# Eighteen passes instead of nineteen: a group's attention laid across two halves of the software pipeline

## The reference

```python
x = _layernorm(x + L0(x, adj))   # five small two-layer GCNs on subsets of the first 25 nodes, fused
x = _layernorm(x + L1(x, adj))   # 8-head attention, scores + log(adj + 1e-6), softmax, output projection
x = _layernorm(x + L2(x, adj))   # relu(D^-1/2 adj D^-1/2 (x W^T + b))
x = _layernorm(x + L3(x, adj))   # 5 gated layers:
    A = (adj != 0)
    for l in range(5):
        m = h @ weight[l];  agg = A^T @ m;  h = gru_cell(agg, h)   # gates r, z, n
```

## Time and profile before

| | |
|---|---|
| median of 3 runs | 1730.95 us (1729.19 to 1732.3) |
| the profiled execution's own time | 1731.32 us |
| its span, first to last instruction | 1729.5 us |
| TensorE busy | 1622.2 us, 94% of the span |
| VectorE / ScalarE / GpSimd busy | 79% / 76% / 45% |
| TensorE weight loads busy | 77% |
| granted TensorE clock over the span | 0.982 of full speed |

### The profile page before, as it was taken

The page is one execution under the profiler, slowest core; times in us unless marked ns, Lnnn a source line. Parts: engine busy times, 40 slices in busy tenths (PEclk is TensorE's granted clock), DMA queues, the critical chain, the costliest instruction groups (busy, mean ns, idle before and its releaser), DMA issues.

```text
span 1729.5 us, 33712 instructions
## 1 busy us (share of the span) xinstructions
PE 1622.2 (94%) x12060; PEld 1328.9 (77%) x12060; DVE 1365.5 (79%) x3531; ACT 1313.4 (76%) x3122; POOL 779.8 (45%) x843
## 2 busy tenths in 40 slices
PE   4779999999999999999999999999999999999984
PEld 3567788787878878787887878788787878877763
DVE  5577897878789787878978787897978789787753
ACT  1467788787778878777887877788787778887763
POOL 2233454535445453544545354454535445453432
PEclk8799999999999999999999999999999999999997
DMA  3000100101010010101001010100101010000000
GB/s 89 21 24 20 30 13 26 29 13 30 25 29 14 26 29 13 30 25 30 14 26 29 14 29 26 29 13 26 28 14 29 26 29 14 25 14 13 13 7 12
DMA packets 84800, 40.92 MB, mean 24 GB/s; under 512 B 10629, under 2 KB 84634, under 8 KB 84634
## 3 DMA queue, kind: packets, MB, share of 16 engines
q1 hardware_dynamic: 84250, 38.64, 8.1%
q10 hardware_dynamic: 384, 0.13, 0.0%
HBM read 30.36 MB, written 8.39 MB: 22 GB/s over the span
## 4 chain that ended last, share of the span: by engine, by line
PE 79%; DVE 11%; ACT 7%; issue 2%; POOL 1%; POOLq 0%; DVEq 0%; ACTq 0%
PE RA L908 17%; PE RB L908 16%; PE Q L875 8%; PE RT L1084 8%; PE RT L875 4%; PE Q L1011 4%; ACT x L510 3%; PE M L875 3%; PE Q L1026 3%; PE M L943 2%; PE M L951 2%; PE Q L994 2%; DVE stats L638 2%; PE M L1054 2%; PE Q L998 2%
## 5 line engine op out<-in xcount | busy, mean ns | idle before, releaser
L493 POOL TENSOR_TENSOR h_lo<-hT,h_hi 128x512 fp32r<-128x512 f32 x160 | 210.5, 1316 | 547.7 <-ACT h_hi L587 518.8
L565 ACT ACTIVATE e_s<-Q,s_ng 128x128 f32<-128x128 f32 x1024 | 296.8, 401 | 19.2 <-DVE s_ng L746 17.4
L496 POOL TENSOR_TENSOR hd<-hT,nn 128x512 f32<-128x512 f32 x160 | 206.2, 1289 | 35.8 <-ACT nn L599 35.7
L593 ACT ACTIVATE tr<-RA,b_rz 128x512 f32<-128x512 f32 x160 | 114.6, 716 | 101.4 <-PE RA L908 101.4
L599 ACT ACTIVATE nn<-tr,wT 128x512 f32<-128x512 f32 x160 | 117.3, 733 | 96.5 <-DVE tr L797 96.5
L752 DVE TENSOR_TENSOR p_s<-Q,adjTe 128x512 f32<-128x512 f32 x256 | 172.0, 683 | 21.7 <-PE Q L875 21.6
L746 DVE TENSOR_REDUCE s_ng<-Q 128x4 f32<-128x512 f32 x256 | 167.8, 681 | 10.1 <-PE Q L1011 8.8
L793 DVE SCALAR_TENSOR_TENSOR un<-tr,un 128x512 f32<-128x512 f32 x160 | 109.7, 685 | 73.3 <-ACT un L596 73.0
L789 DVE TENSOR_TENSOR agg_lo<-RT,agg_hi 128x512 fp32r<-128x512 f32 x160 | 109.9, 687 | 72.0 <-ACT agg_hi L590 70.1
L875 PE MATMUL Q<-ident,e_s 128*128 128x128 f32 x1024 | 156.9, 277 | 9.5 <-ACT e_s L565 9.5
L875 PEld LDWEIGHTS Q<-ident,e_s 128*128 128x128 f32 x1024 | 125.4, 142 | 34.6 <-ACT e_s L565 14.0
(11 more groups left out here) (188 smaller groups left out, 4342.9 us busy)
## 6 DMA issues: line engine op xcount, KB each, us to landing
adjn<-in_adj_dram SPq DMA_DIRECT2D x32, 256.0 KB, 2.9
xin<-in_x_dram SPq DMA_DIRECT2D x32, 256.0 KB, 3.3
adjr<-in_adj_dram SPq DMA_DIRECT2D x32, 256.0 KB, 3.1
out_dram<-x SPq DMA_DIRECT2D x32, 256.0 KB, 2.4
adjc<-in_adj_dram SPq DMA_DIRECT2D x128, 4.0 KB, 1.9
xs<-in_x_dram SPq DMA_DIRECT2D x120, 16.0 KB, 1.7
W1s<-in_L_gnn_W_dram SPq DMA_DIRECT2D x1, 640.0 KB, 4.4
W2s<-in_L_gnn_W_dram SPq DMA_DIRECT2D x2, 320.0 KB, 5.4
```

What stands on the lines that cost most here:

```text
L493: pool.tensor_tensor(h_lo[g][:, :], hT[g][:, :], h_hi[g][:, :], ALU.subtract).then_inc(SG["h_lo"][g], 1)
L496: pool.tensor_tensor(hd[g][:, :], hT[g][:, :], nn[g][:, :], ALU.subtract).then_inc(SG["hd"][g], 1)
L565: ins = act.activation(e_s[:, j, c, :], Q[j][:, c * P:(c + 1) * P], ACT.Exp, bias=s_ng[:, j, c:c + 1])
L593: act.activation(tr[g][:, :], RA[:, :], ACT.Tanh, bias=b_rz[:, 0:1], scale=0.5).then_inc(SG["r_act"][g], 1)
```

## The change

The same steps are laid out with a largest lag of 2. The attention of a group is cut after the first pair of graphs (w = 0): `te` to the first `a` stand at the end of a half, the second pair of graphs and the tail at the start of the next half. The graph convolution of the group follows in that same half, after the attention's tail, and `begin` stands at that half's end; its layers 0 to 2 come in the next half and 3 and 4 in the one after. The small GCNs are done in one half (`l0_deg` to `l0_out`) but for `l0_fuse` and `l0_add`, which come in the next. In all there are 16 + 2 = 18 passes, 36 halves, all of them used. `MERGE` is new for all four engines, `ORDER` is adapted, and the waits for the bank M2 follow the new order of its users. No instruction is added to or taken from the work of a pair.

The diff, without the strings of three engines:

```diff
--- before.py
+++ after.py
@@ -46,46 +46,48 @@
     r_act=LAYERS, u_act=LAYERS, n_act=LAYERS, z_act=LAYERS, rv=LAYERS, rw=LAYERS, h_hi=LAYERS, h_lo=LAYERS, agg_hi=LAYERS, hd=LAYERS, he=LAYERS, h_new=LAYERS,
     f_mm=1, y4=1, ln4=2 * GB, ln4_eps=1, ln4_pow=1, nm4=1, x4=1,
 )
-LAG = 3
+LAG = 2
 
 MERGE = dict(
-    tensor=("AARARRRBBRABARRBRRAARAARAARRBARARBRAARRBBABRRBRBRARRARARRRBARRARAABARABRBAARRRBRRRRAARRRARABAARAAABRRRRA",
-            "AABRRARRRRARRRARRARRBAARARAAARRARARBARABARBRBRRAABRRRAAABARAARRBRARARARRBARRRRARRRRAAAARARBARARRR"),
...
+    tensor=("RABAARBRBRRABRARRRRRRBBABAARABRBRAARAABRRRRARRRAARARARBARBAABARRRBABRRBARAABRARRABRRRRARAARRBAARARBAARARRBR",
+            "ARARRRAAABBRARRAARRAAARBARARARRAAAARRRBABRAAARRARRRRABRRARRRARRBRRARRBARRRRRRARARAAARAARARARRR"),
...
 )
 
 
 def attention_steps(half):
-    at = (1, half)
-    out = [(*at, "te", 0), (*at, "x1_t", 0), (*at, "qkv", 0)]
-    for w in range(PAIRS):
-        out += [(*at, "s", w)]
+    def pair(at, w):
+        out = [(*at, "s", w)]
         for kind, j in (("max", 0), ("max", 1), ("t", 0), ("max", 2), ("t", 1), ("p", 0), ("max", 3), ("t", 2), ("p", 1),
                         ("t", 3), ("p", 2), ("p", 3)):
             out += [(*at, kind, BANKS * w + j)]
-        out += [(*at, "a", w)]
-    return out + [(*at, "u", 0), (*at, "u", 1), (*at, "n", 0), (*at, "n", 1), (*at, "on", 0), (*at, "wo", 0)]
+        return out + [(*at, "a", w)]
+
+    old, new = (1, half), (1 - half, 1 - half)
+    tail = [(*old, "u", 0), (*old, "u", 1), (*old, "n", 0), (*old, "n", 1), (*old, "on", 0), (*old, "wo", 0)]
+    return pair(old, 1) + tail + [(*new, "te", 0), (*new, "x1_t", 0), (*new, "qkv", 0)] + pair(new, 0)
 
 
 def first_third_steps(half):
-    end, last, pair = (1 - half, 1 - half), (2 - half, 1 - half), (0, 0)
-    second = [(*last, "x2_t", 0), (*last, "l2_t", 0), (*last, "l2_agg", 0), (*end, "adj_t", 0), (*end, "l0_add", 0)]
+    end, last, pair = (1 - half, 1 - half), (1, half), (0, 0)
+    first = [(*end, "adj_t", 0), (*end, "l0_add", 0)]
+    third = [(*last, "x2", 0), (*last, "x2_t", 0), (*last, "l2_t", 0), (*last, "l2_agg", 0)]
     if half == 0:
-        return [(*pair, "l0_deg", 0), (*last, "x2", 0), *second, (*pair, "l0_dinv", 0), (*pair, "l0_mask", 0), (*pair, "l0_row", 0),
-                (*pair, "l0_turn", 0), (*pair, "l0_col", 0), (*pair, "l0_nat", 0), (*end, "x1", 0),
-                (*pair, "l0_nat2", 0), (*pair, "l0_y", 0), (*pair, "l0_hid", 0), (*pair, "l0_hid", 1)]
-    return [(*pair, "l0_z", 0), (*pair, "l0_zt", 0), (*pair, "l0_out", 0), (*last, "x2", 0), (*pair, "l0_fuse", 0),
-            *second, (*end, "x1", 0)]
+        return [(*pair, "l0_deg", 0), *first, (*end, "x1", 0), (*pair, "l0_dinv", 0), (*pair, "l0_mask", 0), (*pair, "l0_row", 0),
+                (*pair, "l0_turn", 0), (*pair, "l0_col", 0), (*pair, "l0_nat", 0),
+                (*pair, "l0_nat2", 0), (*pair, "l0_y", 0), (*pair, "l0_hid", 0), (*pair, "l0_hid", 1), *third,
+                (*pair, "l0_z", 0), (*pair, "l0_zt", 0), (*pair, "l0_out", 0)]
+    return [(*pair, "l0_fuse", 0), *first, (*end, "x1", 0), *third]
 
 
 def gated_steps(half):
 
-    this, other, new = (2, half), (3 - half, 1 - half), (2 - half, 1 - half)
+    this, other, new = (2 - half, 1 - half), (2, half), (1, half)
     slots = [(*this, 0), (*other, 3), (*this, 1), (*other, 4), (*this, 2)]
     out = []
     for n, (lag, g, layer) in enumerate(slots):
@@ -383,8 +385,8 @@
                 sp.dma_start(outr[:, b0:b0 + GB, :], x4[g][:, :, :]).then_inc(out_done[g], 16)
 
 
-            ORDER = [(0, 0, "small"), (0, 1, "small"), (3, 0, "store"), (2, 1, "again"), (0, 0, "load"),
-                     (3, 1, "store"), (1, 0, "again"), (0, 1, "load")]
+            ORDER = [(0, 0, "small"), (0, 1, "small"), (0, 0, "load"), (3, 1, "store"), (1, 1, "again"),
+                     (0, 1, "load"), (2, 0, "store"), (0, 0, "again")]
 
             for g in range(NG):
                 sp.sem_inc(out_done[g], 16)
@@ -946,6 +948,8 @@
                         turn_weights() if k == 0 else multiply_weights()
                 elif kind == "l0_z":
                     wait(pe, "hid_t", it, 2)
+                    if it > 0:
+                        wait(pe, "a_relu", it - 1, 1)
                     for c in range(NK):
                         for h in range(2):
                             ins = pe.matmul(group_cols(M2, c), W2s[:, c, h, :], group_cols(hid_t[:, h, :], c), start=(h == 0), stop=(h == 1))
@@ -967,10 +971,12 @@
                     ins.then_inc(S["o_mm"], 1)
                 elif kind == "adj_t":
                     pe.wait_ge(adj_in[g], (it + 1) * 16)
-                    if it == 0:
-                        wait(pe, "o_relu", it, 1) if g == 0 else wait(pe, "y1", it, 1)
+                    if g == 0:
+                        wait(pe, "o_relu", it, 1)
+                    elif it == 0:
+                        wait(pe, "y1", it, 1)
                     else:
-                        wait(pe, "a_relu", it - 1, g + 1)
+                        wait(pe, "a_relu", it - 1, 2)
                     for q in range(GB):
                         ins = turn(M2[:, q * P:(q + 1) * P], adjn[g][:, q, :])
                     ins.then_inc(S["adjt_mm"], 1)
@@ -1043,8 +1049,10 @@
                     ins.then_inc(S["wo_mm"], 1)
                 elif kind == "x2_t":
                     wait(pe, "x2", it, g + 1)
-                    if g == 0 and it + 1 < ITERS:
-                        wait(pe, "o_relu", it + 1, 1)
+                    if it + 1 < ITERS:
+                        wait(pe, "hid_t", it + 1, 2) if g == 0 else wait(pe, "y1", it + 1, 1)
+                    else:
+                        wait(pe, "y1", it, 2) if g == 0 else wait(pe, "a_relu", it, 1)
                     for q in range(GB):
                         ins = turn(M2[:, q * P:(q + 1) * P], x2[g][:, q, :])
                     ins.then_inc(S["x2t_mm"], 1)
```

More of the change, by code:

```diff
@@ L48 @@
 )
-LAG = 3
+LAG = 2
 MERGE = dict(
-    tensor=("AARARRRBBRABARRBRRAARAARAARRBARARBRAARRBBABRRBRBRARRARARRRBARRARAABARABRBAARRRBRRRRAARRRARABAARAAABRRRRA",
-            "AABRRARRRRARRRARRARRBAARARAAARRARARBARABARBRBRRAABRRRAAABARAARRBRARARARRBARRRRARRRRAAAARARBARARRR"),
[L54 to L59, removed]
+    tensor=("RABAARBRBRRABRARRRRRRBBABAARABRBRAARAABRRRRARRRAARARARBARBAABARRRBABRRBARAABRARRABRRRRARAARRBAARARBAARARRBR",
+            "ARARRRAAABBRARRAARRAAARBARARARRAAAARRRBABRAAARRARRRRABRRARRRARRBRRARRBARRRRRRARARAAARAARARARRR"),
+    vector=("RABARABABRRRRAAARRARRRRABRRRAAARRRARRBABRBBBRBARAAAARRBRRABBBRRRABAARRAAABARBAAAARRRRRRBRRABRRRRAAAAABRRBRR",
+            "ARAAARARBABAARRRARAAARRARRRABRAAARARBRRRAARRAARABRRABRARRRARAARRBRRRAAARRBRRRRRRARRRAAARRARARR"),
+    scalar=("RBRABARBRRABRRRRAARARBRAABRBABBARBRARRBRRRAAAARAAARRARRRAABBARRRBABRRRABABRRARARBRRRRARRRAAABARRABAAARARBRR",
+            "ARAAARRRRAAAARAAARBBARRRRARAAAAABRRBARARAARRARRBRRARRRRBRABRRRRARRRRBARARRRRAAAAARAARRARRRARRR"),
+    gpsimd=("RABRARBRAARRRRRBRRRRAABRARBBBARABBRRBARAAARARRABRBARBRRRBRARAAAARBRRRRAABBRRAAAAAARRBAARABRRBAARRRABARRARRR",
+            "AAAARRRRRRRARBRRABBARRRARARABARAAARAAARRRRARAABAAARARRRRRARRABRBARARRARRRARRARRAABAARARRRRRRRA"),
 )
 def attention_steps(half):
-    at = (1, half)
-    out = [(*at, "te", 0), (*at, "x1_t", 0), (*at, "qkv", 0)]
-    for w in range(PAIRS):
-        out += [(*at, "s", w)]
+    def pair(at, w):
+        out = [(*at, "s", w)]
         for kind, j in (("max", 0), ("max", 1), ("t", 0), ("max", 2), ("t", 1), ("p", 0), ("max", 3), ("t", 2), ("p", 1),
```

## The result

The changed kernel takes 1763.51 us (median of four runs, 1763.09 to 1764.85); the kernel before, run beside it, 1731.62 (1729.19 to 1733.11). The ratio is 1.0189, with a 95% interval of 1.0177 to 1.0201: 1.9% slower. The forecast was 1758, with a range of 1722 to 1775. The sum came out right, but two terms of the pass were wrong by a microsecond each and cancelled, as the stages show.

A forecast was written before the change was run, and what follows sets the result against it. The prediction took TensorE, busy for 94% of the span, to bound the kernel. Fill and drain of 311.7 us plus 14 passes of 103.2 gave a span of 1756.5, as a median 1758, range 1722 to 1775.

The forecast's parts named there:

- Fill and drain, 311.7 + 14 P: Whole span: fill of 143.5 us, 14 complete passes of length P, drain of 168.2; P forecast at 103.2.
- the break-even of 101.3: Complete passes: the pass length P at which the changed kernel's span would equal that of the kernel before.
- The three old stalls go, 2.0 us: TensorE in each pass: waits before `u`, `qkv` and `wo` vanish because other steps now stand ahead; 2.0 us gained.
- forecast 98.4: TensorE's work in a complete pass, with the small stalls that stay: 98.4 us, bounds 98.0 and 98.9.
- `begin`, 2.5 us: End of the second half: TensorE waits for x3, three transposes covering part; 2.5 us each pass, bounds 1.9 and 3.0.
- case C: Rival: `begin` chain shorter or partly hidden, no stall between halves; P 100.0, median 1713, range 1700 to 1727; chance 0.2.
- `r0` of g0, 0.9 us: Between first and second half: `r0` waits for agg_hi behind ScalarE's queue, and for agg_lo; 0.9 us, bounds 0 and 2.
- The rest of the pass, put down as covered: All other waits in a complete pass: found covered, often with 0.1 to 0.5 us to spare.
- The clock, 1.4 us: TensorE's clock falls after the `begin` stall in six passes of ten, 2.3 us each; 1.4 per pass on average.
- case B: Rival: the clock holds in the complete passes; P 101.8, median 1738; chance 0.2.
- A: The forecast itself: stall at `begin` and a clock that falls in most passes; 1758, range 1745 to 1775; chance 0.42.

The follow-up runs named there:

- late_all: Changed kernel reordered on VectorE, ScalarE and GpSimd: x3 earlier, finished group's norm split, its output normalisation where ScalarE idles; 1733.1 us, ratio 1.0002.
- late_x3: Changed kernel with VectorE doing the attention's products p1 and p2 ahead of a_bin and nm in the second half; 1818.71 us, ratio 1.0502.
- early_x3: Changed kernel with VectorE's a_bin and shift nm of the next group ahead of the finished group's output norm, both halves; 1759.32 us, ratio 1.0165.
- late_out_only: Changed kernel with ScalarE's four normalisations of the finished group moved into the next half, where ScalarE stands idle; 1757.93 us, ratio 1.0145.
- the pairing named above: Not run: the first half of one follow-up order (52.75 us) with the second half of another (47.52), which would make a pass of 100.3.
- late_relu: Changed kernel with ScalarE's five relus of l0_out after agg_hi of layer 0 in the next half instead of ahead of it; 1781.36 us, ratio 1.0287.

## Why the forecast was right, and where its steps were not

- **Fill and drain, 311.7 + 14 P.** Held as a frame. Measured 316.3: the fill 2.5 us longer (2.2 of it before 105.2, where the forecast had 103), the drain 2.1, with the clock at 0.97 where the kernel before had 1.00. That is 4.6 of the 5.7 us by which the span is above 1756.5. In late_all, with a better order, fill and drain take 145.8 and 166.3, together 312.1; its P of 101.31 is the break-even of 101.3, and its time is that of the kernel before. So at an unchanged P of 100.8 the structure is worth 6 us with the fill and drain of late_all (312.1 + 14 x 100.8 = 1723.3, against 1729.5; the forecast had 6.6), and the order of this change keeps 2 of it (316.3 + 14 x 100.8 = 1727.5).
- **The three old stalls go, 2.0 us.** Right, but TensorE's work was mis-sized: forecast 98.4, measured 99.35. It is not work: the steps `r` take 15.8 us a pass instead of 14.7, with delays that the view counts as busy, 0.5 at `r0` of g0 and 0.4 at `r4` of g1, where each matmul starts within 0.06 us of the end of its `agg_hi` or `agg_lo`. The places where a step follows its own operand closely were not in the forecast's list of waits.
- **`begin`, 2.5 us.** Measured 2.28; late_x3 shows that it is the last wait of its half. That it could be taken away by a shorter chain, as case C had it, was half wrong: early_x3 halved it, and `a0` and `r0` of g1 took what it gave.
- **`r0` of g0, 0.9 us.** Measured 0.55 visible and 0.5 hidden. The chain named was right for the visible half (late_out_only), for the hidden one it is `agg0` followed directly by `r0`.
- **The rest of the pass, put down as covered.** Short by 0.6 us: `turn` 0.33 and `in` 0.29 of layer 2.
- **The clock, 1.4 us.** Mis-sized by 1.0. It fell to 0.50 in four stretches of 14 passes, not in six of ten passes, and each cost about 1.4 us (a first half of 54.27 for 52.92, or 0.4 of the half before and 1.04), not 2.3: 0.4 us a pass. On the clock, case B (it holds) was nearer the truth than A. What made A's number right is luck: 98.4 was as much too low.

The sum with measured terms: 99.35 + 2.28 + 0.55 + 0.62 + 0.05 (three small gaps) + 0.41 = 103.26.

What stays open: why the clock fell in these passes and not in those, though all have the same stalls; and what the pairing named above would take.

## What to carry to other kernels

When a change only moves work in a pipeline that one engine fills, write down for each step the distance to its operand on every engine, also where the profile calls the engine busy: steps that follow their operand closely hide a wait in their length. Before moving work out of a chain, find where its new engine stands idle and for how long; relief for the same wait cost 18 us in a full stretch of ScalarE (late_relu, four more falls of the clock included) and won 6 us in an idle one (late_out_only). And count the two engines beside TensorE as a pair: an order that is better for one of them can stretch the other.
